# Two products per head for the scores of one tile of keys, and a moved rest on GpSimd

## The reference

```python
def _L0_ffn_ref(x, ...):        # weights w * (su @ sv), I = 1792
    a = _anemll_linear(x, gate_w, gate_su, gate_sv)
    b = _anemll_linear(x, up_w, up_su, up_sv)
    return _anemll_linear(jax.nn.silu(a) * b, down_w, down_su, down_sv)

def _L0_attn_ref(x, Wq, Wk, Wv, Wo, q_norm_w, k_norm_w):   # H = 32, HKV = 8, HD = 128
    q, k = _rmsnorm(q, q_norm_w), _rmsnorm(k, k_norm_w)
    scores = jnp.einsum('bkgqd,bksd->bkgqs', qg, k) / math.sqrt(HD)
    bias = jnp.where(rel > 0, NEG_INF, slopes[:, :, None, None] * rel)
    attn = jax.nn.softmax(scores + bias[None], axis=-1)
    out = jnp.einsum('bkgqs,bksd->bkgqd', attn, v)
    return out @ Wo.T

x = x + 0.5 * _L0_ffn_ref(_layernorm(x), ...)
x = x + _L0_attn_ref(_layernorm(x), ...)
x = x + 0.5 * _L0_ffn_ref(_layernorm(x), ...)
```

## Time and profile before

| what | value |
|---|---|
| median of 3 runs | 1238.32 us (1237.34 to 1238.6) |
| the profiled execution | 1237.32 us, span 1236.0 us |
| TensorE busy | 1215.9 us, 98% of the span, 6418 matmuls |
| weight loads | 1065.9 us, 86% |
| VectorE busy | 827.4 us, 67% |
| ScalarE busy | 756.6 us, 61% |
| GpSimd busy | 649.1 us, 53%, and 205.1 us idle ahead of line 1651 |
| granted TensorE clock | 1.00 of full speed (2.4 GHz) |

### The profile page before, as it was taken

How to read it: one execution, slowest core, us unless ns; L and a number is a source line. 1 busy time by engine, 2 the same in 40 slices (tenths; PEclk the granted TensorE clock), 3 DMA queues, 4 the chain that set the end, 5 groups by cost and what they waited for, 6 DMA issues and landing times.

```text
span 1236.0 us, 18593 instructions
## 1 busy us (share of the span) xinstructions
PE 1215.9 (98%) x6418; PEld 1065.9 (86%) x6418; DVE 827.4 (67%) x2002; ACT 756.6 (61%) x1760; POOL 649.1 (53%) x526
## 2 busy tenths in 40 slices
PE   6999999999999999999999999999999999999999
PEld 5788888899998999999999999999999888888887
DVE  7966666676666667667677677667767778655555
ACT  4554442347677767767767767767767764544442
POOL 4696661734676624724824823823824343765550
PEclk9999999999999999999999999999999999999999
DMA  6142322212112122122122122122122010221101
GB/s 232 40 157 106 106 104 102 86 52 85 54 67 103 37 84 94 43 86 94 44 86 86 52 86 86 52 80 93 52 77 86 26 53 17 69 69 52 52 17 68
DMA packets 33453, 93.77 MB, mean 76 GB/s; under 512 B 4113, under 2 KB 4785, under 8 KB 31313
## 3 DMA queue, kind: packets, MB, share of 16 engines
q1 hardware_dynamic: 33120, 92.29, 21.8%
q10 hardware_dynamic: 240, 0.30, 0.1%
HBM read 62.69 MB, written 29.88 MB: 75 GB/s over the span
## 4 chain that ended last, share of the span: by engine, by line
PE 91%; DVE 4%; ACT 2%; POOL 1%; issue 1%; DMA 1%; SPq 0%; DVEq 0%; ACTq 0%; POOLq 0%
PE bank L345 21%; PE bank L347 21%; PE bank L346 21%; PE bank L590 5%; PE bank L424 4%; PE bank L430 4%; PE bank L425 4%; PE bank L604 3%; PE bank L609 3%; PE bank L605 3%; PE bank L569 2%; PE bank L373 1%; DVE stats L1106 1%; PE bank L572 1%; PE bank L361 0%
## 5 line engine op out<-in xcount | busy, mean ns | idle before, releaser
L1651 POOL TENSOR_TENSOR rows<-rows,row_root_y 128x640 f32<-128x640 f32 x64 | 80.6, 1260 | 205.1 <-DVE row_root_y L1102 205.1
L970 ACT ACTIVATE prob<-prob,neg_top 128x128 f32<-128x128 f32 (+3 forms) x256 | 141.2, 553 | 77.0 <-DVE neg_top L1375 76.4
L1645 POOL TENSOR_TENSOR square<-rows 128x640 f32<-128x640 f32 x64 | 79.2, 1254 | 161.0 <-DVE rows L1411 125.1
L1520 POOL TENSOR_TENSOR w_l_late<-raw_late,w_h_late 128x512 fp32r<-128x512 f32 (+1 forms) x59 | 90.5, 1548 | 74.9 <-ACT w_h_late L727 74.9
L979 ACT ACTIVATE prob<-prob,inverse 128x128 f32<-128x128 f32 (+3 forms) x256 | 123.0, 553 | 4.6 <-DVE inverse L1380 4.6
L1386 DVE TENSOR_TENSOR probT_l<-bank,probT_h 128x512 fp32r<-128x512 f32 x160 | 101.4, 683 | 21.8 <-ACT probT_h L985 21.7
L985 ACT CAST probT_h<-bank 128x512 fp32r<-128x512 f32 x160 | 84.6, 596 | 41.9 <-PE bank L590 41.9
L1375 DVE CUSTOM_DVE_ANT_0 prob<-bank,bias 128x128 f32<-128x128 f32 (+3 forms) x256 | 109.7, 484 | 0.0
L1168 DVE SCALAR_TENSOR_TENSOR x_rows<-bank,x_rows 128x512 f32<-128x512 f32 x112 | 75.7, 687 | 45.9 <-PE bank L430 45.9
L345 PE MATMUL bank<-o_h,oT_h 128*128 128x512 f32 x256 | 104.7, 409 | 0.0
L347 PE MATMUL bank<-o_h,oT_l 128*128 128x512 f32 x256 | 100.8, 394 | 0.0
(11 more groups left out here) (213 smaller groups left out, 3747.8 us busy)
## 6 DMA issues: line engine op xcount, KB each, us to landing
x_ring<-x_between SPq DMA_DIRECT2D x64, 256.0 KB, 2.6
x_between<-x_ring SPq DMA_DIRECT2D x56, 256.0 KB, 2.0
raw_late<-w_qkv SPq DMA_DIRECT2D x8, 1536.0 KB, 6.5
raw_early<-ffn_w SPq DMA_DIRECT2D x21, 512.0 KB, 4.0
scaled<-raw_early SPq DMA_DIRECT2D x21, 512.0 KB, 2.7
raw_late<-scaled SPq DMA_DIRECT2D x21, 512.0 KB, 3.7
raw_late<-w_o SPq DMA_DIRECT2D x8, 1024.0 KB, 5.0
x_between<-x_rows SPq DMA_DIRECT2D x8, 256.0 KB, 2.0
```

The source lines that it names most:

```text
L970: last = act.activation(p, p, ACT.Exp, bias=neg_top[:, h:h + 1], scale=-1.0, accum_out=total[:, h:h + 1])
L1520: return pool.tensor_tensor(lo, raw, hi.bitcast(F32), ALU.subtract)
```

## The change

Two things are changed. First, where a unit has one tile of keys (the new in_halves: units 0, 4, ..., 56, but not 60), the scores of a head are two matmuls instead of three. kT_h and kT_l now lie in one tile kT, and one matmul takes both of them as its moving operand (256 columns), the other qT_l with kT_h (128 columns, added onto the first 128). Two heads share a bank, which holds for each head 128 columns of the main sum and 128 of the key rests' part. VectorE adds the latter to the bias for two heads at a time (128x2x128), waits for its own writes, and then does the four reductions as before, with that sum in place of the bias; the bank is released by the second head's reduction, and ScalarE's exponentials wait for that. In these slots VectorE makes turn_rows before pair_roots. Fewer results are taken, so all later banks are numbered otherwise.

Second, GpSimd makes the first block of w_o's rest (o_l of head 0) in a group's slot 0 ahead of norm_rows, not in slot 1, and the rest of the first chunk named for slot 4 (t3) ahead of norm_rows, not behind it.

```diff
--- before.py
+++ after.py
@@ -202,7 +202,9 @@
         rows = sb("rows", [LEAD, G + 2, HD])
         o_h, o_l = sb("o_h", [G, DM], F32R), sb("o_l", [G, DM], F32R)
         v_h, v_l = sb("v_h", [B, TB, HD], F32R), sb("v_l", [B, TB, HD], F32R)
-        kT_h, kT_l = sb("kT_h", [S], F32R), sb("kT_l", [S], F32R)
+        kT = sb("kT", [2, S], F32R)
+        kT_h, kT_l = kT[:, 0, :], kT[:, 1, :]
         qT_h, qT_l = sb("qT_h", [G, P], F32R), sb("qT_l", [G, P], F32R)
         prob = sb("prob", [G, S])
         probT_h, probT_l = sb("probT_h", [TB, G, P], F32R), sb("probT_l", [TB, G, P], F32R)
@@ -307,6 +309,10 @@
         def qkv_place(g, block):
             at = QKV_BLOCKS[g][block]
             return qkv_h[at], qkv_l[at]
+        def in_halves(n):
+            return unit(n)[2] == 0 and n + LEAD < UNITS
         def paired(n):
             return FIRST_PAIRED <= n < UNITS
@@ -576,6 +582,19 @@
                 turned_q, turned_k = results["turn_q", n], results["turn_k", n]
                 pe.wait_ge(evac[turned_q.bank], turned_q.nth)
                 pe.wait_ge(evac[turned_k.bank], turned_k.nth)
+                if in_halves(n):
+                    for h in range(0, G, 2):
+                        r, bank = result("scores", n, h)
+                        for head in (h, h + 1):
+                            cols = (head - h) * 2 * P
+                            pe.matmul(bank[:, cols:cols + 2 * P], qT_h[:, head, :], kT[:, :, 0:P], start=True, stop=False,
+                                      skip_group_check=True)
+                            last = pe.matmul(bank[:, cols:cols + P], qT_l[:, head, :], kT_h[:, 0:P], start=False, stop=True,
+                                             skip_group_check=True)
+                        last.then_inc(full[r.bank], 1)
+                    return
                 for h in range(G):
                     r, bank = result("scores", n, h)
                     last = matmul3(bank[:, 0:keys], (qT_h[:, h, :], qT_l[:, h, :]), (kT_h[:, 0:keys], kT_l[:, 0:keys]), True, True)
@@ -964,7 +983,7 @@
             def exponentials(n, heads):
                 keys = (unit(n)[2] + 1) * P
                 for h in heads:
-                    r = results["scores", n, h]
+                    r = results["scores", n, h - h % 2 if in_halves(n) else h]
                     act.wait_ge(evac[r.bank], r.nth)
                     p = prob[:, h, 0:keys]
                     last = act.activation(p, p, ACT.Exp, bias=neg_top[:, h:h + 1], scale=-1.0, accum_out=total[:, h:h + 1])
@@ -1369,6 +1388,21 @@
             def scores(n):
                 g, _, i = unit(n)
                 keys = (i + 1) * P
+                if in_halves(n):
+                    two = [results["scores", n, h] for h in range(0, G, 2)]
+                    for h, r in zip(range(0, G, 2), two):
+                        dve.wait_ge(full[r.bank], r.nth)
+                        rests = banks[r.bank][:, :].rearrange("p (h m c) -> p h m c", h=2, m=2)[:, :, 1, :]
+                        own_step(dve.tensor_tensor(prob[:, h:h + 2, 0:P], rests, bias[:, h:h + 2, S - P:S], ALU.add))
+                    for h in range(G):
+                        r = two[h // 2]
+                        if h == 0:
+                            own_wait()
+                        last = dve.tensor_tensor_reduce(prob[:, h, 0:P], banks[r.bank][:, h % 2 * 2 * P:h % 2 * 2 * P + P],
+                                                        prob[:, h, 0:P], -(2.0 ** -g), -MASKED, ALU.add, ALU.min, neg_top[:, h:h + 1])
+                        if h % 2:
+                            last.then_inc(evac[r.bank], 1)
+                    return
                 for h in range(G):
                     r = results["scores", n, h]
                     dve.wait_ge(full[r.bank], r.nth)
@@ -1468,11 +1502,15 @@
                 if n % 2 == 0 and paired(n + 2):
                     sum_squares(n + 2)
                     sum_squares(n + 3)
-                if n % 2 == 0:
+                if in_halves(n):
+                    turn_rows(n + 1)
+                if n % 2 == 0 and n + LEAD - 2 < UNITS:
                     pair_roots(n + LEAD - 2)
                 if paired(ahead):
                     add_products(ahead, 2) if n % 2 == 0 else add_products(ahead - 1, 5)
-                turn_rows(n + 1)
+                if n + 1 < UNITS and not in_halves(n):
+                    turn_rows(n + 1)
                 if ahead < FIRST_PAIRED:
                     values_lo(ahead)
                 if n:
@@ -1653,14 +1691,20 @@
             def slot(n):
                 g, at = divmod(n, B * TB)
                 if at == 1:
-                    split_o(g, range(G))
+                    split_o(g, range(1, G))
                 ahead = n + LEAD
                 if n % 2 == 0 and paired(n + 2):
                     square_rows(n + 2)
                     square_rows(n + 3)
                 mixes_now = QKV_MIX_WHEN.get(at, ()) if SEVEN_FROM <= g + 1 < HKV else ()
+                splits = QKV_WHEN[g + 1 >= SEVEN_FROM].get(at, ()) if g < HKV - 1 else ()
                 if at == 4:
                     mix_qkv(g + 1, *mixes_now)
+                    split_qkv(g + 1, *splits[:1])
+                    splits = splits[1:]
+                if at == 0:
+                    split_o(g, (0,))
                 if n + 2 < UNITS:
                     norm_rows(n + 2)
                 if n % 2 == 0 and paired(n + 2):
@@ -1673,8 +1717,7 @@
                     split(1, 0, *(("a11", "a12"), ("a21", "a22"), ("d0", "d1"))[ahead - UNITS])
                 if at == 3:
                     mix_qkv(g + 1, *mixes_now)
-                if g < HKV - 1:
-                    split_qkv(g + 1, *QKV_WHEN[g + 1 >= SEVEN_FROM].get(at, ()))
+                split_qkv(g + 1, *splits)
                 if 0 <= n - LEAD - 1 < PAIRS:
                     token_sums_rest(n - LEAD - 1)
                 if 0 <= n - LEAD < PAIRS:
```

## The result

The changed kernel takes 1250.13 us, the median of 5 runs (1248.68 to 1251.22). The kernel before, run beside it on the same chip, takes 1237.34 us (1236.85 to 1238.6). The ratio is 1.0101, 95% interval 1.009 to 1.0113: slower by 1.0%, 12.8 us. Its profiled execution took 1250.98 us, its span 1249.7.

The account below looks back on a forecast made before the run. TensorE, 91% of the chain, bounds the kernel while other engines deliver in time. Terms 6.9 + 4.5 + 2.3 - 0.4 + 0.8 + 0.4 = 14.5 us gave a median of 1252.8 us, range 1237 to 1259.

Parts of the forecast that it names:

- TensorE's scores: In 15 units with one tile of keys, eight matmuls replace twelve: 0.92 us instead of 1.34, 0.42 less per slot.
- VectorE's additions: Two 128x256 additions ahead of the reductions, 0.41 us each; first reduction 0.79 later, exponentials 1.0 later (bounds 0.6 to 1.6).
- Rival C: The two additions read strided banks at the price of 512 columns (0.69 us each): +21 us, median 1259; chance 0.06.
- The w_qkv chunk slots: Slots 20, 28, 36, 44, 52: GpSimd's chunk rest holds a root step, third head waits; net 1.4 us each, 6.9 in five.
- The extra 0.1 for probT_l: In slots where GpSimd holds the roots, probT_l comes about 0.1 us late for weigh_values, added to the third head's wait.
- The w_o slots: Slots 16, 24, ..., 56: GpSimd's first w_o block holds the roots; wait 1.1 + 0.1, net 0.75 us, 4.5 in six.
- Slots 0 and 1: kT_l has no slack, everything 1.0 us late, roots meet GpSimd's block, probT_l late: +2.3 us (bounds +1.0 to +2.7).
- Slots 8, 9, 12, 13: GpSimd's queue delays the fourth head's load, +0.8 us; a kT_l wait of 0.43 goes but the chunk holds roots, +0.4.
- no charge: Slot 24: norm_rows starts later, last three o_l blocks end near 570.3, just ahead of a late TensorE; priced at nothing.
- Rival A: Roots not delayed by GpSimd's rests, or the held bank doesn't matter: -3.8 us, median 1234.5; chance 0.18.
- Rival B: Only the w_qkv chunk collides; roots are through before GpSimd's w_o block matters: +7.5 us, median 1245.8; chance 0.14.

Follow-up runs that it names:

- e7: Changed kernel, t3's rest back behind norm_rows, scratch memset, subtraction or copy on GpSimd in its place; one run: slots +0.97 (memset), +1.67 and +1.69 (subtraction), +1.47 (copy).
- e5: Changed kernel with the addition of products ahead of the roots in slots of one tile of keys: 1249.04 us, ratio 1.0098.
- second execution: The changed kernel profiled once more, unaltered, to check the granted clock: 1248.11 us, slot 1 +1.28.
- e1: Changed kernel with both GpSimd moves undone; two products per head and turn_rows ahead of the roots stay: 1239.47 us against 1237.08, ratio 1.0014.
- e11: Changed kernel with both GpSimd moves undone and the values' rests moved behind the rest TensorE waits for: 1232.81 us against 1237.25, ratio 0.9966.
- e2: Kernel before with the two GpSimd moves alone: 1248.57 us, ratio 1.0085.

## Why the prediction was right, and where its terms were off

**The mechanism and the sum.** Predicted 1252.8, measured 1250.13: the kernel before, run beside it, was 1.0 lower than the base of the sum, and the change costs 12.8 us instead of 14.5. The path stood in the profile as told: a root step held by GpSimd's rest (e7), the addition of products late behind it, the third head's scores of the next slot waiting, and VectorE's queue behind that (e5).

That the slots of the profiled execution add up to 14.5 us, as predicted, is luck. The two large terms were too big by 3.0 us (6.9 against 5 x 1.08 = 5.4, and 4.5 against 3.0), and a clock that the prediction didn't have put 1.6 + 1.3 us in their place. In the second execution, with the full clock there, the same slots add up to 11.5.

**TensorE's scores.** 0.92 us and 0.42 less per slot, as worked out; a moving operand in two runs of 128 columns costs no more here than one of 256.

**VectorE's additions.** Priced 0.41 each and 0.33 apart, and so measured (the row of 0.74 merges the two); the first reduction starts 0.78 after the first addition (0.79 predicted). Rival C falls. oT_l was in time as said. The prediction let the additions meet GpSimd's subtraction for t4; in the trace they lie beside square_rows (510.71 to 513.18), and last 0.41 all the same.

**The w_qkv chunk slots: mis-sized, 1.4 predicted, 1.08 measured.** The wait was taken as 1.7 + 0.1 and was 1.50 in all. The error is which root step is held. I held the step that begins at 8.91 into the slot, with GpSimd starting at 8.93; the trace shows that step through (519.13, 0.05 ahead of GpSimd's start at 519.18) and the next one held. One step more is done before the hold, 0.2 us. The trace of the kernel before has such a case: beside the GpSimd instruction that starts at 253.49, the step that was held is the one at 253.64, while the one 0.05 us ahead of the start went through:

```profile
253.44 0.16 DVE L1102 SCALAR_TENSOR_TENSOR ln_root_y<-ln_root_b,ln_root_y 128x4 f32<-128x4 f32 x1
```

The extra 0.1 for probT_l cost nothing: its load waits 0.19 us, but loads run ahead of their matmuls, and the load behind it is as late as the ones before probT_l (1.47 against 1.46 us).

**The w_o slots: mis-sized, 0.75 predicted, 0.50 measured.** The same error: held was the tenth of eleven, with one behind it (0.2 us), where I had two behind. GpSimd's block started 0.06 us later in the slot than I had it, and the ninth step, 0.04 us ahead of it, went through. And the 0.1 again.

**Slots 0 and 1.** Predicted +2.3. In the second execution they are +2.28. In the first they are +3.89, of which 1.6 is the clock, which the prediction didn't hold possible.

**Slots 8, 9, 12, 13.** Predicted +0.8 and +0.4, measured +0.71 and +0.41.

**What the prediction did not see.** Its path is right and its account of the cause is incomplete. It priced the late roots only for VectorE's queue and what the bank releases, and wrote of norm_rows in slot 24 "no charge". e1 shows that the late roots, with no step held, cost 0.96 us in each chunk slot and 0.50 in each w_o slot, through norm_rows and the rests behind it on GpSimd. The GpSimd moves take that wait away and put a larger one in its place. Of the 10.4 us between the changed kernel and e1, the held steps are 8.7; the rest is about what the clock takes in some of the runs (last section). Because of this gap I forecast e1 at 1232.3 instead of 1239.5. Rival A as a whole (roots undisturbed while the rests are early) can't be had by undoing an edit and was not tried.

Rival B falls: the additions cost what was priced, the roots still had two steps to go when GpSimd started, and all six w_o slots hold a step.

## What to carry to other kernels

When a chain of short VectorE steps on data in SBUF is on the path, count GpSimd's long reading instructions beside it: the first step that begins behind the start of one grows to its end (1.73 us beside 1.86, 1.15 beside 1.28), while a step that had begun 0.04 to 0.06 us ahead went through. A later place for such a chain must be priced at each engine that its end releases, and in the order of their queues; here reordering GpSimd's rests behind the chain by urgency (e11) gained 6.7 us over e1, where filling its idle time ahead of the chain lost 8.6. Idle time that an engine spends waiting for another is free only if what fills it doesn't slow the one waited for.

## What the hardware did that I had not expected

The granted clock of TensorE fell after a short idle stretch, in some executions of the same program. The changed kernel, slots 1 and 2, by windows of a microsecond; the columns are time, length, busy share and count of PE, PEld, DVE, ACT and POOL, the granted clock, and the DMA share and rate:

```profile
278.00:279.00 1.00, 0.01 (x1) 0.00 (x0) 0.86 (x6) 0.00 (x0) 0.00 (x0) 1.00 0.00 0
279.00:280.00 1.00, 0.20 (x1) 0.21 (x2) 1.00 (x5) 0.00 (x0) 0.98 (x1) 1.00 0.03 8
280.00:281.00 1.00, 1.00 (x6) 0.96 (x6) 1.00 (x7) 0.89 (x3) 1.00 (x2) 1.00 0.00 0
281.00:282.00 1.00, 1.00 (x5) 1.00 (x5) 0.59 (x3) 1.00 (x5) 1.00 (x2) 0.56 0.00 0
282.00:283.00 1.00, 1.00 (x5) 1.00 (x4) 1.00 (x3) 0.68 (x4) 1.00 (x2) 0.50 0.00 0
283.00:284.00 1.00, 1.00 (x7) 0.90 (x6) 0.03 (x1) 0.94 (x3) 1.00 (x2) 0.50 0.00 0
284.00:285.00 1.00, 1.00 (x6) 1.00 (x6) 0.00 (x0) 1.00 (x3) 1.00 (x1) 0.74 0.00 0
```

TensorE stood idle for 1.79 us up to 279.80 (and for 1.2 us up to 275.85), worked for 1.3 us at the full 2.4 GHz, and then ran at 0.50, the level of 1.2 GHz, from about 281.1 to about 284.5. The same stretch in the second execution, with the same idle 1.79 us, shows the full clock:

```profile
281.00:282.00 1.00, 1.00 (x7) 1.00 (x6) 0.59 (x3) 1.00 (x4) 1.00 (x2) 1.00 0.00 0
282.00:283.00 1.00, 1.00 (x10) 0.96 (x9) 1.00 (x2) 0.83 (x4) 1.00 (x2) 1.00 0.00 0
283.00:284.00 1.00, 1.00 (x8) 1.00 (x7) 0.18 (x2) 0.78 (x2) 1.00 (x1) 1.00 0.00 0
```

Of five profiled executions with that idle stretch in slot 1 the clock fell in two (the changed kernel and e7), for 1.6 us of time each; of the seven with 0.75 us of idle or less at the same load of probT_l, in none. In slot 13 of e2 it fell a microsecond behind 2.06 us of idle. Around the start of slot 62, where all twelve have the same two waits (0.65 us late in slot 61, and 0.84 us up to slot 62), it fell in five, for 1.3 to 1.55 us. So a wait near 2 us can cost nearly twice its length. What decides between two executions with the same waits is open.

The mean granted clock on record for each run shows the same over more runs. The changed kernel took 1248.11 and 1248.68 us in its runs at 1.000, 1250.07 and 1250.13 at 0.999, and 1250.98 and 1251.22 at 0.997. The kernel before, beside the experiments, took 1236.03 to 1237.53 us in 19 runs at 1.000, and all but two of its 15 runs at 0.999 took 1238.39 to 1239.34. At the full clock the change thus costs some 11.4 us, by slots 11.5, and about 1.4 of the 12.8 between the medians is the clock.
